# Third attention: rows split into fp16 halves on GpSimd, loads three batches ahead, another order of work

## What is computed

```python
def _mha(q_in, k_in, v_in, wq, bq, wk, bk, wv, bv):
    B, Sq, _ = q_in.shape
    Sk = k_in.shape[1]
    def split(x, S):
        return x.reshape(B, S, H, HD).transpose(0, 2, 1, 3)
    Q = split(q_in @ wq + bq, Sq)
    K = split(k_in @ wk + bk, Sk)
    V = split(v_in @ wv + bv, Sk)
    scores = jnp.einsum('bhqd,bhkd->bhqk', Q, K) / HD ** 0.5
    probs = jax.nn.softmax(scores, axis=-1)
    ctx = jnp.einsum('bhqk,bhkd->bhqd', probs, V)
    return ctx.transpose(0, 2, 1, 3).reshape(B, Sq, D)
...
x = _ln(x + _mha(x, ctx, ctx, ...), ln2_g, ln2_b)   # x: (16, 224, 512), ctx: (16, 750, 512), 16 heads of 32
```

## Time and profile before

| | |
|---|---|
| time, median of 3 runs | 3676.26 us (3672.01 to 3680.65) |
| profiled execution | 3677.58 us, span 3675.7 us |
| PE, DVE, ACT, POOL busy | 88%, 75%, 58%, 21% of the span |
| mean granted TensorE clock | 0.942 |
| third attention | about 1200 to 2675 us of the span |
| DMA | 309 MB, 84 GB/s |

### The profile page before, as it was taken

How to read it: one execution, slowest core, us unless ns; L and a number is a source line. 1 busy time by engine, 2 the same in 40 slices (tenths; PEclk the granted TensorE clock), 3 DMA queues, 4 the chain that set the end, 5 groups by cost and what they waited for, 6 DMA issues and landing times. The chain is left out here.

```text
span 3675.7 us, 90205 instructions
## 1 busy us (share of the span) xinstructions
PE 3250.3 (88%) x36535; PEld 2545.2 (69%) x36576; DVE 2750.3 (75%) x4907; ACT 2114.0 (58%) x4664; POOL 788.6 (21%) x802
## 2 busy tenths in 40 slices
PE   7999999599997599899999999999708999999995
PEld 4999997489996377777777777777606565656562
DVE  4788887489997588888888888888753666666666
ACT  2666666277776266667776677667633343434442
POOL 0111111045555002111111112111201221212121
PEclk9999999799997799999999999999759999999998
DMA  2333432344442433333333333332151000000000
GB/s 92 110 114 97 120 95 86 114 124 133 130 135 89 125 93 101 92 90 89 95 103 89 89 94 101 92 89 79 46 190 48 24 24 30 24 29 24 29 18 18
DMA packets 218498, 309.30 MB, mean 84 GB/s; under 512 B 64900, under 2 KB 138628, under 8 KB 217447
## 3 DMA queue, kind: packets, MB, share of 16 engines
q1 hardware_dynamic: 218086, 303.53, 27.8%
HBM read 212.45 MB, written 90.64 MB: 82 GB/s over the span
## 5 line engine op out<-in xcount | busy, mean ns | idle before, releaser
L759 ACT ACTIVATE cross_p_hi<-cross_ps 125x448 f16<-125x448 f32 x768 | 416.8, 543 | 260.2 <-PE cross_ps L714 249.0
L822 DVE TENSOR_TENSOR cross_p_lo<-cross_ps,cross_p_hi 125x448 f16<-125x448 f32 x768 | 473.9, 620 | 102.7 <-ACT cross_ps L760 93.9
L815 DVE TENSOR_REDUCE cross_mx<-cross_ps 128x1 f32<-128x750 f32 x512 | 476.7, 931 | 48.9 <-PE cross_ps L680 45.5
L760 ACT ACTIVATE cross_ps<-cross_ps 125x448 f32<-125x448 f32 x768 | 417.6, 544 | 0.0
L680 PE MATMUL cross_ps<-cross_qk_stack 96*128 96x375 f16 x1024 | 258.5, 334 | 71.5 <-DMA cross_qk_stack<-cross_spill 41.3
L1268 PE MATMUL ffn_ps_f<-ffn_xt,ffn_f_hi 128*128 128x256 f16 x1792 | 300.9, 275 | 10.4 <-DVE ffn_xt L1408 5.0
L602 PE MATMUL cross_ps<-cross_w_hi,cross_ct 128*125 128x128 f16 x3072 | 298.4, 222 | 0.0
L714 PE MATMUL cross_ps<-cross_qk_stack 97*125 97x224 f16 x1536 | 284.4, 273 | 3.8 <-DMA cross_qk_stack<-cross_mrow 2.8
L602 PEld LDWEIGHTS cross_ps<-cross_w_hi,cross_ct 128*125 128x125 f16 x3072 | 284.1, 138 | 0.3
L1284 PE MATMUL ffn_ps_c<-ffn_f_hi,ffn_ht 128*128 128x512 f16 x896 | 284.1, 379 | 0.0
L602 PE MATMUL cross_ps<-cross_w_lo,cross_ct 128*125 128x128 f16 x1536 | 275.5, 221 | 0.0
(11 more groups left out here) (260 smaller groups left out, 9480.6 us busy)
## 6 DMA issues: line engine op xcount, KB each, us to landing
cross_spill<-cross_proj SPq DMA_DIRECT2D x64, 487.0 KB, 2.8
cross_qk_stack<-cross_spill SPq DMA_DIRECT2D x128, 243.5 KB, 3.7
cross_c_rows<-ctx SPq DMA_DIRECT2D x48, 500.0 KB
causal_spill<-causal_proj SPq DMA_DIRECT2D x64, 224.0 KB, 2.0
causal_qk_stack<-causal_spill SPq DMA_DIRECT2D x128, 112.0 KB, 2.2
self_spill<-self_proj SPq DMA_DIRECT2D x64, 224.0 KB, 2.0
self_qk_stack<-self_spill SPq DMA_DIRECT2D x128, 112.0 KB, 2.2
cross_qk_stack<-cross_spill SPq DMA_DIRECT2D x64, 187.5 KB, 4.1
```

The lines of the kernel that those rows point to most:

```text
L759: act.activation(p_hi[:, n % 4, :], scores, ACT.Exp, scale=EXP_SCALE)
L760: act.activation(scores, scores, ACT.Exp, scale=EXP_SCALE).then_inc(exp_done, 1)
L815: dve.tensor_reduce(mx[:, place(b, g), t, h:h + 1], ps_qk[:, :, 0:KT // 2], AX.XY, ALU.max).then_inc(max_done, 1)
L822: dve.tensor_tensor(p_lo[:, n % 4, :], ps_st[0:KC, st_bank(g, n), 0:2 * T], p_hi[:, n % 4, :], ALU.subtract).then_inc(lo_done, 1)
```

## The change

In the third attention alone:

- GpSimd multiplies the rows of x and of the context by 16 in place, writes their fp16 rounding and their fp16 rest (`x_parts`, `c_parts`): two tensor_scalar and one tensor_tensor for x, and the same for each of three context parts (`split x`, `split c`).
- TensorE transposes both halves as fp16 into one PSUM bank (L638), twice as many transposes. ScalarE copies both halves in one instruction, VectorE does nothing for them, and the bank is free after ScalarE's copy.
- `load` and `loadc` run three batches ahead and wait for the split that empties the buffer. The prologue loads batches 0, 1 and 2 and splits 0 and 1.
- `ORDERS["cross"]` is another: q, k0 and k1 stand in the first half of each unit; x0 and x1 move from group 0 to group 1.
- `o`, `z` and `yn` share their memory with the staging buffer (`cross_early`), which makes room for the halves.

The self-attentions change in form only: a semaphore's count is worked out in another way.

```diff
-    "cross": (("E1 q M0 S2 loadc residual load row S3 k0a M1 V0 S4 k0b x0 V1 M2 S5 V2 S6 x1 k1a V3 M3 S7 V4 k1b V5 "
-                 "M4 S8 E0 v0a M5 S9 V6 V7 spill S10 V8 M6 S11 v0b S0 V9 V10 M7 S1 v1 V11 stack",
...
+    "cross": (("E1 q M0 S2 S3 V0 k0a M1 V1 k0b V2 M2 S4 k1a M3 k1b spill S5 M4 load row S6 V3 S7 v0a S8 V4 V5 E0 M5 "
+                 "v0b S9 residual V6 V7 V8 M6 S10 S11 v1 V9 M7 S0 stack S1 V10 V11 splitx",
+                 "E1 S2 k0a k0b M0 norm q M1 S3 row S4 S5 V0 V1 k1a M2 V2 V3 k1b apply S6 V4 S7 V5 v0a M3 E0 S8 S9 V6 "
+                 "M4 v0b V7 M5 S10 V8 S11 V9 x0 M6 S0 v1 x1 V10 spill stack M7 V11 S1 splitc0 c0 loadc0",
...
             yield "weights", Batch(0), 0, 0
             yield from loads(1)
+            if cross:
+                yield from splits(1)
+                yield from loads(2)
             yield from unit(0)
...
         def job_scale(kind):
-            return S_ACT if kind[0] in "xco" else RESPLIT
+            return 1.0 if kind in PARTS_JOBS else S_ACT if kind[0] in "xco" else RESPLIT
...
-                    wait_apart(sp, proj_full, b.val(lambda k: job_index["x1", k - 2, 0] + 1 if k >= 2 else 0),
-                               passed)
+                    if cross:
+                        wait(sp, x_split, max(b.first - 1, 0))
...
-                    wait_apart(sp, proj_full, b.val(lambda k: job_index[last, k - 1, 0] + 1 if k >= 1 else 0), passed)
+                    wait(sp, c_split, 3 * (b.first - 1) + part + 1 if b.first >= 1 else 0)
...
-                            pe.wait_ge(c_rows_in[int(kind[1]) // 2], b.val(lambda k: 16 * (k + 1)))
-                        last = transposes(bank, KC, [(c_rows[:, int(kind[1]), :], DC, 0)])
+                            pe.wait_ge(c_split, 3 * b.first + int(kind[1]) // 2 + 1)
+                        last = part_transposes(bank, KC + 1, [(i, c_parts[:, i, int(kind[1]), :], DC, 0)
+                                                              for i in range(2)])
...
-                    else:
+                    elif kind not in PARTS_JOBS:
                         dve.wait_ge(proj_hi, b.val(lambda k: hi_index[kind, k, g] + 1))
...
+                elif kind == "split c":
+                    last, chunks = f"c{2 * n + 1}", slice(2 * n, 2 * n + 2)
+                    pool.wait_ge(c_rows_in[n], 16 * (b.first + 1))
+                    wait(pool, proj_full, job_index[last, b.first - 1, 0] + 1 if b.first >= 1 else 0)
+                    rows = c_rows[:, chunks, :]
+                    pool.tensor_scalar(rows, rows, S_ACT, 1.0, ALU.mult, ALU.mult).then_inc(c_hi_done, 1)
+                    pool.wait_ge(c_hi_done, 6 * b.first + 2 * n + 1)
+                    pool.tensor_scalar(c_parts[:, 0, chunks, :], rows, 1.0, 1.0, ALU.mult, ALU.mult).then_inc(c_hi_done, 1)
+                    pool.wait_ge(c_hi_done, 6 * b.first + 2 * n + 2)
+                    pool.tensor_tensor(c_parts[:, 1, chunks, :], rows, c_parts[:, 0, chunks, :], ALU.subtract
+                                       ).then_inc(c_split, 1)
```

More of the change, by code:

```diff
@@ L333, in loads, with splits @@
                     yield "load c", Batch(b), 0, n
+            def splits(b):
+                yield "split x", Batch(b), 0, 0
+                for n in range(3):
+                    yield "split c", Batch(b), 0, n
             def unit(u):
@@ L340, in prologue @@
             yield from loads(0)
+            if cross:
+                yield from splits(0)
             yield from inputs(0)
@@ L414, in attention @@
                 job_index[kind, b.first, g] = len(job_index)
+                job_list.append((kind, b.first, g))
+                if kind not in PARTS_JOBS:
+                    free_index[kind, b.first, g] = len(free_index)
                 if kind not in UNSPLIT_JOBS:
@@ L466, in all_projected @@
         def all_projected(b, g):
[L468 removed]
+            return max(free_index[kind, b.first, g] + 1 for kind in UNIT_JOBS if kind[0] in "qk")
         def stack_count(b, g, own):
@@ L586, in _, with part_transposes @@
             pe.wait_ge(const_dve, 1)
+            def part_transposes(bank, n, tiles):
+                out = ps_proj[:, bank, :].bitcast(F16)
+                for i, rows, chunks, at in tiles:
+                    for c in range(chunks):
+                        k, to = rows.shape[0], (i * chunks + c) * n + at
+                        last = pe.transpose(out[:, to:to + k], rows[:, c * P:(c + 1) * P], ident16[0:k, 0:k])
+                return last
             def transposes(bank, n, tiles):
@@ L882, in perform @@
             def perform(kind, b, g, n):
-                if kind == "evacuate" and n == 1:
+                if kind == "split x":
+                    pool.wait_ge(x_rows_in[b.par], 32 * (b.first // 2 + 1))
+                    wait(pool, proj_full, job_index["x1", b.first - 1, 0] + 1 if b.first >= 1 else 0)
+                    rows = x_rows[:, b.par, :, :]
+                    pool.tensor_scalar(rows, rows, S_ACT, 1.0, ALU.mult, ALU.mult).then_inc(x_hi_done, 1)
+                    pool.wait_ge(x_hi_done, 2 * b.first + 1)
+                    pool.tensor_scalar(x_parts[:, 0, :, :], rows, 1.0, 1.0, ALU.mult, ALU.mult).then_inc(x_hi_done, 1)
+                    pool.wait_ge(x_hi_done, 2 * b.first + 2)
+                    pool.tensor_tensor(x_parts[:, 1, :, :], rows, x_parts[:, 0, :, :], ALU.subtract
+                                       ).then_inc(x_split, 1)
+                elif kind == "split c":
[9 more added lines that the diff above has]
+                                       ).then_inc(c_split, 1)
+                elif kind == "weights":
+                    if norm is not None:
+                        pool.wait_ge(gain_in, 32)
+                    if biases is not None:
+                        pool.wait_ge(v_bias_in, 16)
+                elif kind == "evacuate" and n == 1:
                     pool.wait_ge(pv_evac, no(b, g, 2, 2))
```

98 lines of the change are left out of this document (67 added, 31 removed), and 10 rows, old and new, of the table ORDERS.

## The result

The changed kernel takes 3619.82 us (median of 4 runs, 3609.36 to 3625.05) against 3678.45 us before (3672.01 to 3681.41): ratio 0.9839, 95% interval 0.9812 to 0.9866, some 59 us faster. The prediction was 3610 in 3552 to 3672. The profiled execution took 3625.05 us, its span is 3623.2.

A forecast was written before the change was run, and what follows sets the result against it. TensorE, busy 92% of the cross loop, was taken as the bound, its waits as lost time. From 3677.6 us: -41.0 - 41.3 - 40 + 2 + 28 + 10 + 10 + 6 = -66.3, 3611.3, adjusted to 3610; range 3552 to 3672.

The forecast's parts named there:

- start of the stage: Third attention before its loop: batch 0's splits and a later first spill delay the first M0, +6 us.
- x wait: Cross loop: TensorE's wait for the transfer of x rows goes, as they load a batch earlier, -41.0 us.
- stack wait: Cross loop: the wait for the stack transfer ahead of the row-maximum matmuls goes entirely, -41.3 us.
- lower clock: Cross loop: with both waits gone, the causes of TensorE's slow clock go, -40 us.
- transposes: Cross loop, TensorE: twice as many fp16 transposes cost about the same as fp32 ones, +2 us over 14 batches.
- ScalarE's longer copies: Cross loop: copying both halves overfills the second half of a unit, 2 us a batch, +28 us in all.
- c0 waits for GpSimd: Cross loop, group 1: split c0 ends at 19.4 us, wanted at about 19.3; charged 0.7 us a batch, +10.
- small waits, denser order: Cross loop: new small waits of a denser order, VectorE working 66 of 80 us a batch, +10 us.
- rival 1: Full gain: p buffers absorb ScalarE's clumps, split c0 is in time, none of 48 us given back: 3562 us; chance 0.17.
- rival 3: GpSimd too slow: at 2.35 us a tensor_scalar, c0 waits 2.8 us in each of 14 batches: 3684 us; chance 0.09.
- Rival 4: Contention: GpSimd's new 18.4 us a batch hold up VectorE in the cross loop: about 3700 us; chance 0.04.
- Rival 2: Waits change place: TensorE waits for the maximum and for banks instead, at twice the charge: 3658 us; chance 0.15.

The follow-up runs named there:

- all_late_c0_first: all_late with GpSimd's split of context chunks 0 and 1 moved ahead of norm and apply: 3584.65 us, ratio 0.9747 to the kernel before.
- x_early: The kernel before with only the rows of x loaded three batches ahead instead of two: 3603.65 us, ratio 0.9800.
- all_late: The changed kernel with batch 2's prologue loads behind the first two units' stacks, loadc1 and loadc2 behind their groups' stacks: 3582.28 us, ratio 0.9746 to the kernel before.
- old_order_split: The changed kernel with the order of before, split and load tokens put in: 3716.34 us, ratio 1.0092 to the kernel before.
- split_longer: The changed kernel with a second, identical copy in each GpSimd split, 1.04 us more: 3663.98 us, ratio 0.9956 to the kernel before.
- loads2_late: The changed kernel with the prologue's loads of batch 2 behind the first two units' spills and stacks: 3606.43 us, ratio 0.9795 to the kernel before.

## Why the prediction was right

The sum came out, 3610 against 3619.82, but by luck: most of its terms were wrong, and they cancel. In the loop two (stack, clock) promised 44 us too much and four (ScalarE, c0, small waits, transposes) charged 47 too much; the start of the stage cost 12 us more than charged. In the loop, in us:

| term | predicted | measured |
|---|---|---|
| x wait | -41.0 | -41.0 |
| stack wait | -41.3 | -14.4 (26.9 left) |
| lower clock | -40 | -23 (TensorE's busy time 1236.9 to 1213.6) |
| transposes | +2 | -1 (at full clock, 54.0 to 53.3) |
| ScalarE's longer copies | +28 | 0, no wait of TensorE for ScalarE is listed |
| c0 waits for GpSimd | +10 | 0, by the waits and all_late_c0_first |
| small waits, denser order | +10 | +4 (maxima 21.7 to 29.0, others 4.3 to 1.2) |
| loop | -72.3 | -72.0 |

The measured column adds up to within 4 us of its total: the change of the transposes is also in TensorE's busy time, and pauses too short for the list of waits are in no row.

- **x wait**: right, and proven by one edit: x_early has it alone. Its worth was more than its length, in that kernel 69 us of loop for 41 of wait. The prediction counted this clock in a term of its own and for both waits together.
- **Stack wait**: the step that failed is "also where a context load of 500 KB stands between spill and stack". The prediction took the 8.8 us from spill to M0 out of a row without such a load and used it for the places with one. There it is 14.7 us, more than the new order leaves, because the stack's transfers land 10.3 us after their issue instead of 5.6. It named loadc0 as SyncE's wait for GpSimd and missed loadc1, whose wait has the stack behind it. The prediction's reserve (half of the 41 us stays) was nearly what happened. loadc1 and loadc2 moved behind the stack take 20 us of it away.
- **Lower clock**: mis-sized because the stack's pauses stayed. With them gone (all_late) TensorE is busy for 1203 us, 34 less than before, near the 40. An estimate from the traces (each matmul's start to next start, without waits, against the mean of its shape at full clock) puts what the lower clock cost at 43.5 us of the loop before, 16.4 in the changed kernel and 7.0 in all_late. So it gave back 27 us, not 23; the new order took some 5 back by standing further apart, 8.5 in the value matmuls alone. The prediction had no term for that.
- **ScalarE**: the size of a copy was right (1.015 us, predicted 1.01), the step from there was not. A unit's second half being 0.4 us too full was charged as 2 us a batch, though ScalarE's mean load of 75% (962 of 1276 us) left it room to catch up; no wait of TensorE for ScalarE is in the loop's list. What rival 1 said for itself, the 70% load, was the better argument.
- **c0**: predicted 0.1 us late, observed just on time. The walk along GpSimd's queue was right to some tenths: old_order_split shows what happens when it doesn't fit (75 us of waits), split_longer that there is no slack.
- **Start of the stage**: +18 instead of +6. Two steps failed, each by some 5 us. The chain of splits of batch 0 was worked out as if all rows were there. GpSimd stood for 1.79, 2.05 and 1.39 us until each context piece of batch 0 landed, so it ended at 1224.7, not 1221.7; and batch 1's rows were issued at 1234.6, not at the 1231.0 of the walk, so its splits ended at 1260.3, not 1256.6, and the spill left 62.1 us after the stage's first load instead of 57.1. And the spill was given its old landing time, while three context loads of 500 KB stood ahead of it: 9.3 us until the stack instead of 4.05. Nearly all of it hangs on the loads ahead of the spill: with them moved (loads2_late) the start is 90.4 us, 1.4 above before, so the later chain of batch 0 by itself costs no more than that. The bound that the prediction named as "wrong" for the first M0, 1272 us, was passed (1275.2), and two of its signs of being right failed: the stack's wait is 26.9 us, not under 10, and the loop's clock 0.98, not 0.99.
- **GpSimd and contention**: the lower end of the price, 1.04 us, was measured to the hundredth, and with it rival 3 fell for this kernel. Rival 4 fell: 620 ns for VectorE's subtraction, while GpSimd works twice as long as before in the loop (462 against 231 us). The Trainium skill's rule (SBUF: State Buffer, Who interferes with whom) that a VectorE instruction with at most one SBUF input, outside the two-port modes, doesn't contend with GpSimd agrees with this.
- **Rival 1** (3562) is where the kernel would be without its misplaced loads, nearly: all_late reaches 3582. **Rival 2** was half of what is seen: the stack's wait stayed at 27 us, but the maxima took only 7 more.

## What to carry to other kernels

A small transfer that an engine waits for (here spill and stack, two hops that take some 9 us together) is better not issued behind or around a bulk load on the same queue: look at each load's place among SyncE's instructions, since its cost shows under the small transfer's name. Three places here cost 34 us of 3620. When a change has several parts, make the smallest alone: two edits that load x rows a batch earlier gave 75 us, the whole change 59. A wait of TensorE of a few us cost more than its length here (13 of them, 41 us in all, cost 69 in the loop), as the matmuls behind it ran at the lower clock, so price it with what follows.

## What was not expected of the hardware

- GpSimd's two-input operation on 1024 columns takes 2.13 us with an fp16 second operand and fp16 output, against 2.35 us in fp32.
- From a spill to its stack it took 2.8 to 2.9 us as a rule with no load ahead of it (single ones up to 5.1), 6.3 us behind one context load and two stores, and 9.3 us behind three context loads. With a context load between the two, the stack's issue is hardly later (2.95 us), but its last transfer lands 10.3 us after the first one's issue instead of 5.6.
- 1.04 us more on GpSimd in each split, where nothing had waited for it, cost the kernel 44 us: 12.5 of waits for the split, 10 for the stack, 13.5 of TensorE's busy time, 6 at the start of the stage; the rest was not traced.
